# An attention kernel's row maxima, turned on VectorE and brought into the stack by four transfers of ScalarE's queue

## The reference

```python
q, k, v = heads(xn @ Wq.T) * 32 ** -0.5, heads(xn @ Wk.T), heads(xn @ Wv.T)
logits = einsum('abhqc,abhkc->abhqk', q, k) + bias[:, None]     # layer 1 adds a mask term
weights = softmax(logits, axis=-1)
wavg = einsum('abhqk,abhkc->abhqc', weights, v)
gate = sigmoid(xn @ Wg.T + gating_bias)
x = x + (gate * wavg) @ Wo.T + bo
```

## Time and profile before

| | |
|---|---|
| time, median of 3 runs (lowest to highest) | 3687.65 us (3685.44 to 3690.11) |
| the profiled execution's own time | 3685.48 us |
| its span in the profile | 3683.7 us |
| busy: PE, DVE, POOL, ACT | 95%, 94%, 83%, 79% |
| granted TensorE clock, mean | 0.993 |
| transfers issued: SP's queue, ACT's queue | 252.90 MB, 200.33 MB |

### The profile page before, as it was taken

One profiled execution on the slowest core, in us unless ns is written; L12 is line 12 of the kernel. 1 busy time (PEld: TensorE's weight loads), 2 busy tenths in 40 slices (PEclk: granted clock), 3 DMA queues, 4 the chain that ended last, 5 costly groups with the idle time before them and its releaser, 6 DMA issues.

```text
span 3683.7 us, 123322 instructions
## 1 busy us (share of the span) xinstructions
PE 3485.9 (95%) x36360; PEld 2625.5 (71%) x36360; DVE 3467.2 (94%) x11679; ACT 2892.0 (79%) x5393; POOL 3039.3 (83%) x2076
## 2 busy tenths in 40 slices
PE   0699999999999999999969999999999999999997
PEld 0577777777777777777737777777777777777775
DVE  7799999999999999999949999999999999999997
ACT  0588888888888888888847778777778777877875
POOL 3488888888888888888847888888888888888887
PEclk9999999999999999999989999999999999999998
DMA  9555555555555555555535556655666566655663
GB/s 381 148 121 115 115 116 119 116 115 116 117 117 115 117 115 119 115 115 116 114 113 115 117 117 118 120 118 117 118 118 119 117 118 116 122 116 117 118 121 74
DMA packets 454996, 454.09 MB, mean 123 GB/s; under 512 B 43136, under 2 KB 445696, under 8 KB 454416
## 3 DMA queue, kind: packets, MB, share of 16 engines
q1 hardware_dynamic: 247120, 252.90, 38.6%
q10 hardware_dynamic: 207808, 200.33, 19.7%
HBM read 182.39 MB, written 67.24 MB: 68 GB/s over the span
## 4 chain that ended last, share of the span: by engine, by line
PE 92%; DVE 2%; DMA 2%; issue 1%; SPq 1%; POOL 1%; ACT 1%; DVEq 0%; ACTq 0%; POOLq 0%
PE proj_b L769 19%; PE proj_a L769 18%; PE av_bank L796 14%; PE max_bank L780 13%; PE exp_bank L785 12%; PE proj_a L823 9%; PE den_bank L803 6%; PE proj_b L814 2%; DVE stats L613 1%; DMA k_stack<-k_lo 1%; DMA probs<-in_xT 1%; SPq L349 0%; DVE max_bank L683 0%; POOL probs_sum L449 0%; DVE probs L695 0%
## 5 line engine op out<-in xcount | busy, mean ns | idle before, releaser
L683 DVE CUSTOM_DVE_ANT_0 max_bank<-max_bank,bias_q 128x256 f32<-128x256 f32 x4096 | 1647.5, 444 | 147.0 <-PE max_bank L780 124.6
L449 POOL TENSOR_TENSOR probs_sum<-probs 128x1024 f32<-128x1024 f32 x512 | 1208.3, 2360 | 290.8 <-ACT probs L473 154.1
L695 DVE TENSOR_TENSOR probs<-exp_bank,bias_k 128x512 f32<-128x512 f32 x2048 | 1397.1, 682 | 7.5 <-PE exp_bank L785 7.5
L780 PE MATMUL max_bank<-k_stack,q_stack 96*128 96x256 f16 (+1 forms) x4096 | 787.0, 273 | 14.6 <-DMA k_stack<-k_lo 11.7
L785 PE MATMUL exp_bank<-q_stack,k_stack 100*128 100x256 f16 x4096 | 782.2, 272 | 10.2 <-DVE probs L695 7.6
L473 ACT ACTIVATE probs<-probs,mask_bias 128x1024 f32<-128x1024 f32 x512 | 572.8, 1148 | 60.3 <-DVE probs L695 60.2
L683 DVE DVE_READ_ACCUMULATOR2_ANT row_max<- 128x1 f32 x4096 | 580.2, 142 | 0.0
L476 ACT ACTIVATE probs<-probs 128x1024 f32<-128x1024 f32 x512 | 525.2, 1054 | 51.2 <-DVE probs L695 51.2
L796 PE MATMUL av_bank<-probs,v_sb 128*32 128x256 f32 x8192 | 549.1, 385 | 3.1 <-ACT probs L473 1.6
L780 PEld LDWEIGHTS max_bank<-k_stack,q_stack 96*128 96x128 f16 (+1 forms) x4096 | 380.7, 98 | 166.6 <-DVE row_max L683 105.8
L785 PEld LDWEIGHTS exp_bank<-q_stack,k_stack 100*128 100x128 f16 x4096 | 394.2, 97 | 72.9 <-DVE probs L695 12.7
(11 more groups left out here) (134 smaller groups left out, 7064.4 us busy)
## 6 DMA issues: line engine op xcount, KB each, us to landing
q_stack<-q_hi SPq DMA_DIRECT2D x512, 128.0 KB
k_stack<-k_hi SPq DMA_DIRECT2D x512, 128.0 KB
q_stack<-q_lo SPq DMA_DIRECT2D x256, 128.0 KB
k_stack<-k_lo SPq DMA_DIRECT2D x256, 128.0 KB
y<-in_xT ACTq DMA_DIRECT2D x128, 256.0 KB, 2.9
layer_out<-y ACTq DMA_DIRECT2D x128, 256.0 KB, 2.7
y<-layer_out ACTq DMA_DIRECT2D x128, 256.0 KB, 2.9
out<-y ACTq DMA_DIRECT2D x128, 256.0 KB, 3.2
```

The lines of the kernel that those rows point to most:

```text
L449: pool.tensor_tensor(probs_sum[:, g], pr[:, :, 0, :], pr[:, :, 1, :], ALU.add).then_inc(sum_ready, 1)
L683: op = dve.tensor_tensor_reduce(out=max_bank[h % 2][:, t, :], in0=max_bank[h % 2][:, t, :], in1=bias_q[:, h, t, :], scale=1.0 / FINE, scal ...
L695: dve.tensor_tensor(probs[:, r.ring(2), h], exp_bank[h % 2][:, :, :], bias_k[:, h], ALU.add).then_inc(logits_ready, 1)
L780: op = pe.matmul(bank_[:, t, :], q[0:n, t * P:(t + 1) * P], k[0:n, :], start=True, stop=True)
```

## The change

The maxima don't go through PE any more. DVE turns them itself, 32 x 32 block by block, from `row_max` (now 16 columns for each row, repeated twice) into 32 columns of `proj_b`'s bank. Of those it makes a scaled float16 copy and a scaled float32 copy, and of the two, both pieces at once: in each block of 32 partitions the lower 16 hold one piece, the upper 16 the other, by a column of constants (`piece_scale`). All four operations are 128 partitions by 32 columns. ACT's `coarse` is gone. The pieces of a row then lie in four blocks of 32 partitions by 32 tokens, so four transfers, one for each block, bring them into partitions 98 and 99; each moves 32 runs of 32 float16 values (64 bytes). They are issued from ACT's stream, in front of `split(s, 0)`. SP keeps the transfer of the constant rows in layer 1.

Besides, the last row of each layer is treated apart: its denominators are formed by PE from both key tiles without POOL's `probs_sum`, its `gated`, `gated_lo` and residual are made by DVE, and in the slots after a layer's last row ACT makes `gated_hi` ahead of the store of y.

```diff
-        shift_ps = pb[0:HEADS, 0, :]
+        max_turned, max_kept = pb[:, 0, 0:2 * HEADS * TT], pb[:, 0, 2 * HEADS * TT:4 * HEADS * TT]
...
# SyncE
-                    wait(sp, coarse_ready, r.count(1, 1), sp_passed)
-                    sp.dma_start(stack[0][MASK_ROW + 2:MASK_ROW + 3, i], coarse[:, b]).then_inc(shift_in[i], 16)
-                    wait(sp, fine_ready, r.count(1, 1), sp_passed)
-                    sp.dma_start(stack[0][MASK_ROW + 3:MASK_ROW + 4, i], fine[:, b]).then_inc(shift_in[i], 16)
...
# ScalarE, between the exponentials' tiles
-                    act.wait_ge(shift_psum, r.count(1, 1))
-                    q = r.plus(-2)
-                    wait(act, shift_in[q.ring(4)], shift_full(q))
-                    act.activation(coarse[:, i], shift_ps, ACT.Copy, scale=-FINE / COARSE).then_inc(coarse_ready, 1)
...
# ScalarE, ahead of split(s, 0)
+                r = s.plus(-2)
+                if r.active():
+                    i, b = r.ring(4), r.ring(2)
+                    wait(act, exp_psum, r.plus(-4).count(8, 8))
+                    wait(act, pieces_ready, r.count(1, 1), act_passed)
+                    for p in range(P // HC):
+
+                        act.dma_start(stack[0][MASK_ROW + 2:MASK_ROW + 4, i].rearrange(
+                            "w h (t p e) -> w (h t) p e", p=P // HC, e=HC)[:, :, p],
+                            pieces[HC * p:HC * (p + 1), b]).then_inc(shift_in[i], 16)
...
# VectorE
-            def fine_shift(r):
-                i = r.ring(2)
+            def turn_maxima(r):
+                dve.wait_ge(max_done, r.count(8, 8))
+                if r.plus(1).active():
+                    dve.wait_ge(gate_ready, r.plus(1).count(1, 1))
+                dve.transpose(max_turned.rearrange("p (w j) -> p w j", w=2),
+                              row_max[:, r.ring(2)].unsqueeze(1).broadcast_to([P, 2, HEADS * TT])).then_inc(max_turn, 1)
+
+            def coarse_pieces(r):
+                dve.wait_ge(max_turn, r.count(1, 1))
+                dve.tensor_scalar(coarse[:, :], max_turned, -FINE / COARSE, None, ALU.mult)
+                dve.tensor_scalar(max_kept, max_turned, piece_scale[:, 1:2], None, ALU.mult).then_inc(coarse_ready, 1)
+
+            def shift_pieces(r):
                 dve.wait_ge(coarse_ready, r.count(1, 1))
-                dve.scalar_tensor_tensor(out=fine[:, i], in0=coarse[:, i], scalar=COARSE / FINE, in1=shift_ps,
-                                         op0=ALU.mult, op1=ALU.add).then_inc(fine_ready, 1)
+                dve.scalar_tensor_tensor(out=pieces[:, r.ring(2)], in0=coarse[:, :], scalar=piece_scale[:, 0:1],
+                                         in1=max_kept, op0=ALU.mult, op1=ALU.add).then_inc(pieces_ready, 1)
...
# TensorE
-            def maxima_rows(r):
-                pe.wait_ge(max_done, r.count(8, 8))
-                if r.plus(1).active():
-                    pe.wait_ge(gate_ready, r.plus(1).count(1, 1))
-                wait(pe, fine_ready, r.plus(-1).count(1, 1))
-                i = r.ring(2)
-                for t in range(TT):
-                    op = pe.transpose(shift_ps[:, t * P:(t + 1) * P], row_max[:, i, t], ident[:, :])
-                op.then_inc(shift_psum, 1)
...
-                        wait(pe, fine_ready, s.plus(-2).count(1, 1))
+                        wait(pe, pieces_ready, s.plus(-2).count(1, 1))
```

More of the change, by code:

```diff
@@ L75, in active, with last @@
         return not isinstance(self.turns, int) or 0 <= self.off < ROWS
+    def last(self):
+        return isinstance(self.turns, int) and self.off == ROWS - 1
     def index(self):
@@ L398, in slot @@
                 r = s.plus(-5)
-                if r.active():
+                if r.active() and not r.last():
                     b = r.ring(2)
@@ L487, in split, with high_gated @@
                 act.activation(qk_f32[m][:, b], ps[:, :, :], ACT.Copy, scale=scale).then_inc(qk_f32_ready[m], 1)
+            def high_gated(r):
+                if r.active():
+                    b = r.ring(2)
+                    act.wait_ge(gated_ready, r.count(1, 1))
+                    wait(act, out_psum, r.plus(-2).count(1, 1))
+                    act.activation(gated_hi[:, b], gated[:, b], ACT.Copy).then_inc(gated_hi_ready, 1)
             def slot(s):
@@ L575, in slot @@
                         op.then_inc(stats_ready, 1)
[L576 to L581, removed]
+                if s.active():
+                    high_gated(s.plus(-4))
                 if s.active():
@@ L676, in maxima @@
             def maxima(r, h):
+                of = r.plus(-1)
                 i = r.ring(2)
@@ L730, in slot @@
                         maxima(s.plus(-1), step)
+                    if step == 0 and s.plus(-2).active():
+                        turn_maxima(s.plus(-2))
                     if step == 3 and s.plus(-4).active():
@@ L736, in slot @@
                         logits(r, h)
-                    if step == 1 and s.plus(-2).active():
-                        fine_shift(s.plus(-2))
+                    if step == 0 and s.plus(-2).active():
+                        coarse_pieces(s.plus(-2))
+                    if step == 0 and s.plus(-2).active() and not s.plus(-1).active():
+                        shift_pieces(s.plus(-2))
                     r = s.plus(-4)
@@ L746, in slot @@
                             turn_reciprocal(r)
+                        if step == 4 and r.last():
+                            last_gated(r)
+                    r = s.plus(-5)
+                    if step == 4 and r.last():
+                        last_residual(r)
             for l in range(2):
@@ L798, in average @@
                 op.then_inc(av_psum, 1)
[L799 removed]
+                if not r.last():
+                    pe.wait_ge(sum_ready, r.count(2, g + 1))
                 if g == 0:
                     wait(pe, den_left, r.plus(-1).count(1, 1))
[L802 to L815 removed]
+                parts = [probs[:, r.ring(2), 4 * g:4 * (g + 1), t, :] for t in range(TT)] if r.last() else [probs_sum[:, g]]
+                for t, part in enumerate(parts):
+                    for j in range(4):
+                        op = pe.matmul(den_bank[HC * j:HC * (j + 1), g, :], ones[:, :], part[:, j, :],
+                                       start=(t == 0), stop=(t == len(parts) - 1))
+                op.then_inc(den_psum, 1)
             def output(r, o):
@@ L829, in slot @@
                 for step in range(8):
-                    r = s.plus(-2)
-                    if step == 1 and r.active():
-                        maxima_rows(r)
                     r = s.plus(-1)
```

62 lines of the change are left out of this document (40 added, 22 removed).

## The result

The changed kernel takes 3942.43 us (median of 4 runs, 3941.56 to 3943.9) against 3687.9 us for the kernel before on the same chip: a ratio of 1.0691, 95% interval 1.0672 to 1.0709. It is slower, by the mechanism that was forecast, and by 149 us more than the forecast of 3793.

What follows compares the result with a forecast made beforehand. PE and DVE, both near their limit and waiting for each other, bound the kernel. 3685.5 + 118 (0.47 us more per slot, times 252, from PE's stall) - 10 (last rows) = 3793 us; own range 3700 to 3880, whole 3572 to 3930.

Steps and rivals of the forecast that it cites:

- PE's own slot: PE's time per row: 13.62 us less 0.22 for two turning matmuls and 0.26 waiting for `fine`, giving 13.14 us.
- DVE's four operations: New 128x32 operations on DVE: 0.15 us each, 0.60 together, for a DVE slot of 13.23 us.
- The path over DVE to PE does not get longer through them: Three of DVE's four new operations fall into step 0, where DVE has 0.40 us to spare, so no lengthening.
- The start of the issues: ACT sees the pieces and starts issuing 1.16 us after PE starts the maxima of head 1.
- The price of an issue: Each of ACT's four issues takes c = 0.60 us start to start, bounds 0.24 and 0.74; no change at 0.48.
- From the last issue to q_hi: On ACT, about 0.1 us for the waits of `q_hi` after the four issues.
- The stall: PE waits for `q_f` before the output projection: 4c - 1.45, 0.95 us at c = 0.60, slot 14.09 us.
- The last row: Treating each layer's last row apart saves 6 us at the end and 4 between layers: -10 us, between -3 and -13.
- The landing was hidden: The pieces' transfers land before PE asks for them, unless landing takes over 3.4 us; a load takes 2.9.
- The cheap issue: Rival: ACT's issues cost 0.28 to 0.39 us, stall at most 0.11 us, 3582 us; chance 0.37.
- The rival of dearer issues: ACT's issues at 0.74 us, slot 14.65, 3935 us; chance 0.12 shared with DVE as bound and late landing.
- signs of being wrong: On ACT: issues taking under 0.45 us, or starting well before 1.16 us after PE starts head 1's maxima.

Runs made afterwards that it cites:

- one issue: Changed kernel with only the first of its four transfers of pieces, issued on ACT, three quarters of the shift left out: 3571.5 us, ratio 0.9686.
- the ten forms: Changed kernel plus ten groups of four issues, each another form of transfer, on ACT behind each layer's end: 3980.11 us, a single run.

## Why the prediction was wrong, step by step

- **PE's own slot**, 13.14 us: measured 13.17 behind the stall and 13.16 with one issue. Right. Both pieces, the turning matmuls and the wait for `fine`, came off.
- **DVE's four operations**, 4 x 0.15 = 0.60 us: their starts to the next start are 0.13, 0.09, 0.16 and 0.16, together 0.54 to 0.55. Right in size. "The path over DVE to PE does not get longer through them" was wrong. They stand right ahead of the maxima of head 1 (L718 until 1011.75), which DVE starts 0.78 us after PE does instead of the 0.57 of the earlier trace rows. The 0.40 us "to spare" behind the L695 of step 0 was used up and 0.21 more. The three operations there take only 0.38 us. What was left out is that DVE waited in that gap for PE's maxima of head 1, and these come 0.22 us sooner once the two turning matmuls ahead of them are gone: 0.38 + 0.22 - 0.40 = 0.20. The prediction took the 0.22 us off PE's slot and still counted it as DVE's spare time. The estimate of 191 ns for each comes from the Trainium skill, "VectorE: DVE Perf Modes", The TRN2 errata — SBUF-src ops pay a fixed extra latency per instruction, whose formula is given there for an fp32 `tensor_tensor` of 512 and 2048 columns. The rows have 180 to 250 ns long and 90 to 160 ns to the next start, so the starts, which make the slot, are nearer to my row than to the page.
- **The start of the issues**, +1.16 us: 1012.34 is +1.46. 0.21 of it is DVE's late start, the rest mostly the operation on the pieces, 0.24 us long where I had about 0.17.
- **The price of an issue**, c = 0.60: measured 2.60 / 4 = 0.65 us. I had argued for it by partitions laid out anew, from 0.55 and 0.70, with 0.60 for two in a row; the ten forms show that this argument was wrong, and that on ACT's queue an issue from SBUF into the stack is 0.61 to 0.64 us, plus the gap, in all seven forms tried. Four times 0.05 is 0.20 us.
- **From the last issue to q_hi**, 0.10: 1015.13 - 1014.94 = 0.19.
- **The stall**, 0.95 us: `q_hi` at +4.25 instead of +3.66, 0.59 late, of which 0.10 comes back because PE started the projection 0.06 us behind `q_f`, without the tenth that I had allowed for weights. So 1.43 us. This is the step that failed: not the mechanism but the size of "PE's stall is 4c - 1.45". The constant has the larger part, 0.30 + 0.09 - 0.10 = 0.29 us, and c the other 0.20. Slot 14.60 instead of 14.09: 0.51 x 252 = 129 of the 149 us.
- **The last row**, -10 us, 6 and 4: the 6 us at the end are right, 7.1 by the treatment alone and 6.7 in the changed kernel. The 4 us between the layers are not shown: 3.4 in one run at a higher clock, 0.7 in another, and -1.0 in the changed kernel. All that is beside the slots came to about +4 us instead of -10; about 5 us of that are lost in the first rows of the layers, beyond their stalls. With 252 times the 0.015 us between 13.62 and 13.605, that is 18 of the remaining 20 us.
- **The landing was hidden.** Right: PE waited 10 times for the pieces, 13.9 us in all, in the whole run, and with the issues behind `q_f` a transfer landed about 2.6 us after its issue started, not over 3.4.
- **The rivals.** The cheap issue was wrong: four take 2.60 us, and PE waits for what stands behind them. The Trainium skill, "DMA: Bandwidth & Descriptors", Issuing engines are not separate DMA queues, calls that time usually small relative to the DMA. This case's trace agrees with the comparison, 0.62 us against about 2.6 to landing, but not with what the rival drew from it: the transfer runs beside ACT, and the issue holds ACT. The sum for c = 0.44 in that rival was wrong too: 4 x 0.44 - 1.45 = 0.31 gives a slot of 13.45 and 3633 us, not 3645. The rival of dearer issues gave 3935 us, near the result, by c = 0.74, which no issue on ACT had at the median: a number that fits is no proof of its step.
- **The range** ended at 3930, 12 us short. It held the bounds of c alone and none for when the issues can start, though a late start goes into the stall in full. Of the signs of being wrong neither came, since both looked to a smaller stall; none was named for a larger one.

## What to carry to other kernels

Where an engine computes and also issues transfers, write down its order as one stream and price an issue like an operation: here 0.65 us each, 2.6 us in front of the one result for which PE waits. A gap is worth what its end allows: two issues nearly fitted, the third and fourth cost about their full time. When issues move to another queue, look at what stands behind them there too, and close the loop: the same four issues on SP made a loop of 13.71 us through landing, maxima and pieces, while one on ACT and three on SP came within about 0.1 us of PE's own slot once the constant rows stood first. In such a sum, the moment when the chain starts needs a bound of its own, as much as the price of a link. And where an engine's spare time is a wait for work that the same change moves forward, that time goes with the change.

## What the runs showed of the hardware

- On ACT's queue, an issue from SBUF into the stack takes 0.61 to 0.64 us in seven forms, 0.65 start to start in a row of four; from SBUF to DRAM 0.44; two 4 KB rows from a DRAM input 0.27. On SP's queue 128 partitions into 32 take 0.55.
- The releaser named for ACT's longest wait (`q_hi` <- `exp_bank`, 666.9 us) does not account for it: ACT's queue was issuing, and with one issue the wait is put down to PE's q projection (`proj_a`), 228.5 us in all. A row like [2.97 <-PE exp_bank L833] is to be read beside the queue's rows of the same stretch.
- Short DVE operations of 128x32 last 0.18 to 0.25 us, but the next operation starts 0.09 to 0.16 us after their own start.
